# Second set loaded inside the first set's first layer, that layer on 32x32 tiles of TensorE, the sum M on 64x32 tiles, loops written out

## What is computed

```python
def _gn(v):                      # per image and channel
    return (v - mean(v, (1, 2))) / sqrt(var(v, (1, 2)) + 1e-5)

# layer 0: w1 (32, 4), wg (4, 32, 32), w2 (32, 4)
y = gelu(x[..., None] * w1)
z = gelu(einsum('bhwim,moi->bhwmo', y, wg))
out = einsum('bhwmc,cm->bhwc', z, w2)
# layer 1: 4x4 depthwise FIR filter
# layer 2: in windows of 8x8, keys times queries: attn = einsum('bxyhcp,bxyhdp->bxyhcd', q, k) * temperature
# layer 3: weights of 3x3 patches from x itself, scattered back; then batch norm and leaky ReLU
x = x + layer0(_gn(x)); x = x + layer1(_gn(x)); x = x + layer2(_gn(x)); x = x + layer3(_gn(x))
```

## Time and profile before

| | |
|---|---|
| median of 3 runs | 1093.64 us (1091.95 to 1094.71) |
| the profiled execution | 1092.42 us |
| its span | 1090.2 us |
| instructions | 20559 |
| mean granted TensorE clock | 0.845 |
| busy: TensorE, VectorE, ScalarE, GpSimd | 828.1, 821.3, 579.5, 319.2 us |
| data moved | 36.27 MB, 33 GB/s |

### The profile page before, as it was taken

One profiled execution on the slowest core, in us unless ns is written; L12 is line 12 of the kernel. 1 busy time (PEld: TensorE's weight loads), 2 busy tenths in 40 slices (PEclk: granted clock), 3 DMA queues, 4 the chain that ended last, 5 costly groups with the idle time before them and its releaser, 6 DMA issues. The chain is left out here.

```text
span 1090.2 us, 20559 instructions
## 1 busy us (share of the span) xinstructions
PE 828.1 (76%) x6876; PEld 574.6 (53%) x6876; DVE 821.3 (75%) x1165; ACT 579.5 (53%) x615; POOL 319.2 (29%) x233
## 2 busy tenths in 40 slices
PE   5699994979997648635999949979986487445654
PEld 4343334978885448124433319968875384023433
DVE  7577888987876854788577888978758835979993
ACT  5799992333333226445999943323332172525553
POOL 0000006700007940330000029200029900526665
PEclk9799997999998759558899978989998687558686
DMA  9100000000000000225000000000000000003556
GB/s 296 52 0 0 0 0 1 1 1 1 0 0 3 1 20 0 78 65 167 0 0 0 0 0 2 0 2 1 0 1 2 1 20 0 1 0 116 154 155 193
DMA packets 51403, 36.27 MB, mean 33 GB/s; under 512 B 1697, under 2 KB 50977, under 8 KB 51361
## 3 DMA queue, kind: packets, MB, share of 16 engines
q1 hardware_dynamic: 51360, 35.71, 10.7%
HBM read 18.93 MB, written 16.78 MB: 33 GB/s over the span
## 5 line engine op out<-in xcount | busy, mean ns | idle before, releaser
L343 PE MATMUL ps<-work,cst 128*128 128x512 f32 x512 | 237.3, 611 | 17.3 <-ACT work L556 13.5
L343 PEld LDWEIGHTS ps<-work,cst 128*128 128x128 f32 x512 | 94.7, 193 | 158.8 <-issue 144.6
L556 ACT ACTIVATE work<-X,l0s 128x2048 f32 (+1 forms) x64 | 136.7, 2141 | 3.8 <-SPq L303 3.8
L563 ACT ACTIVATE work<-ps 128x2048 f32<-128x2048 f32 x64 | 123.1, 1924 | 8.5 <-PE ps L343 8.3
L999 POOL TENSOR_TENSOR work<-cst,ksum 128x512 f32<-128x512 f32 x64 | 69.6, 1107 | 175.0 <-SPq L303 172.4
L787 DVE TENSOR_TENSOR work<-ps,cst 64x512 f32<-64x512 f32 x128 | 88.2, 689 | 37.1 <-PE ps L410 35.3
L964 POOL TENSOR_TENSOR co<-mv,cst 128x1 f32<-128x1 f32 x8 | 1.5, 191 | 384.5 <-DVEq L250 298.3
L585 ACT ACTIVATE work<-ps 128x512 f32<-128x512 f32 x80 | 47.8, 597 | 98.6 <-PE ps L363 98.6
L374 PE MATMUL ps<-cst,work 128*128 128x143 f32 x640 | 95.9, 294 | 1.4 <-DVE X L737 1.1
L262 PE MATMUL ps<-ST,work 32*128 32x512 f32 x256 | 59.0, 1013 | 45.9 <-DVE work L923 20.4
L707 DVE SCALAR_TENSOR_TENSOR work<-work,cst 128x2048 f32<-128x2048 f32 x32 | 75.2, 2351 | 24.5 <-ACT work L563 24.3
(11 more groups left out here) (96 smaller groups left out, 1548.0 us busy)
## 6 DMA issues: line engine op xcount, KB each, us to landing
work<-x SPq DMA_DIRECT2D x32, 512.0 KB, 4.8
out<-work SPq DMA_DIRECT2D x64, 256.0 KB, 3.2
work<-choose SPq DMA_DIRECT2D x8, 128.0 KB, 2.7
cst<-consts SPq DMA_DIRECT2D x1, 1009.5 KB, 9.2
cst<-consts SPq DMA_DIRECT2D x1, 64.0 KB, 1.9
```

Source lines behind the costliest of these rows:

```text
L343: last = pe.matmul(ps[:, 4 * (m % 2) + b, :], wg[:, m, :], yb[:, m, b * BANK:(b + 1) * BANK], start=True, stop=True)
L556: act.activation(yb[:, m, :], X[:, ds(s * PIX + i * CHUNK, CHUNK)], ACT.Gelu, scale=l0s[:, m:m + 1], bias=l0s[:, MULTI + m:MULTI + m + 1]) ...
L563: act.activation(zb[:, m % 2, :], ps[:, 4 * (m % 2):4 * (m % 2) + 4, :].rearrange("p a b -> p (a b)"), ACT.Gelu).then_inc(s_zs, 1)
```

## The change

- **Load of set 1.** Stage 0 runs for set 0 only. In set 0's stage 1, SP brings set 1 in one-bank pieces (4 columns of the width, 256 KB, two buffers), GpSimd lines each up, TensorE transposes it into bank 6 or 7, VectorE takes its moments and copies it to X. GpSimd works out set 1's scales there too. There is one barrier less.
- **First layer on tiles.** `project_y` uses 16 tiles of 32x32: row tile g is image g, column tile k4 is a quarter of the unit's pixels. z then lies in banks 0 to 3 with one image per bank. There is one such buffer, not two. The products with w2 and the sum over m move from VectorE to TensorE: `weigh_z` multiplies each half unit with diagonal 32x32 matrices (`diag`) on 8 tiles and accumulates in banks 4 and 5. VectorE adds each half chunk of 1024 columns from PSUM to X (`add_half`). `zb` has five buffers, `yb` two.
- **M on 64x32 tiles.** The two windows of a pair go to two row tiles with 33 columns each (32 keys and a one) in place of 128 columns with zeros. `kh` needs no clearing, and the keys' bias is one instruction on 128 partitions.
- **Loops written out.** `Fori` loops become Python loops, so each engine's program is straight. `ksum` lies in the shared work space. The first use of the gelu table is asked for at the end of stage 7.

```diff
-RING, DEEP = 2, 4
+RING, DEEP, ZDEEP = 2, 4, 5
...
-        yb, _e = part(0, [DEEP, CHUNK])
-        zb, _e = part(_e, [RING, CHUNK])
-        acc, _ = part(_e, [CHUNK])
+        yb, _e = part(0, [RING, CHUNK])
+        zb, _e = part(_e, [ZDEEP, G, BANK])
+        stage_b, _e = part(_e, [RING, G, 4 * C])
+        lined_b, _ = part(_e, [RING, 4, G, C])
...
-        kh, _e = part(_e, [RING, 4, G, P])
+        kh, _e = part(_e, [RING, 4, G, C + 1])
 
         rs, _e = part(_e0, [RING, NWIN, P])
-        qb, _ = part(_e, [RING, WS, NWIN // 2, WS])
+        qb, _e = part(_e, [RING, WS, NWIN // 2, WS])
+        ksum = work[:, _e:_e + NWIN * NWIN]
...
-            eng.wait_ge(s_stage, s * (STAGES * ENG) + (k + 1) * ENG)
+            eng.wait_ge(s_stage, (s * (STAGES - 1) + k + 1) * ENG)
...
-                for k in range(STAGES):
+                for k in range(1 if s else 0, STAGES):
+                    if k == 1 and s + 1 < NS:
+                        for n in range(NB):
+                            if n >= RING:
+                                sp.wait_ge(s_lined_b, n - RING + 1)
+                            sp.dma_start(stage_b[:, n % RING, :, :],
+                                         x[(s + 1) * G:(s + 2) * G, :, 4 * n:4 * n + 4, :].rearrange("g h w c -> h g (w c)")
+                                         ).then_inc(s_load_b[n % RING], 16)
                     if k == 5:
                         for r in range(TILES):
                             sp.dma_start(sel[C * r:C * r + C, :, :], choose[0:C, 0:GROUPS, :]).then_inc(s_sel, 16)
-                    if k == 7 and s + 1 < NS:
-
-                        for u in range(LOADS):
-                            load(s + 1, u, u)
...
+                def project_y(i, m):
+
+                    k = s * UNITS + i * MULTI + m
+                    pe.wait_ge(s_y, k + 1)
+                    if k:
+                        pe.wait_ge(s_zs, k)
+                    for k4 in range(4):
+                        for g in range(G):
+                            rows = slice(C * g, C * g + C)
+                            last = pe.matmul(ps[C * k4:C * k4 + C, g, :], wg[rows, m, C * g:C * g + C],
+                                             yb[rows, m % 2, k4 * BANK:(k4 + 1) * BANK], start=True, stop=True)
+                    last.then_inc(s_zp, 1)
+
+                def weigh_z(i, m, hf):
+
+                    n, k = s * (PIX // CHUNK) + i, s * UNITS + i * MULTI + m
+                    pe.wait_ge(s_zs, k + 1)
+                    if m == 0 and 2 * n + hf:
+                        pe.wait_ge(s_x1, 2 * n + hf)
+                    for g in range(G):
                         for b in range(2):
-
-                            pe.wait_ge(s_bank, s * NB + i * 8 + (2 * u + b + 1))
-                            for w in range(4):
-                                one_w = lined[:, u % 2, 4 * b + w, :, :].rearrange("p g c -> p (g c)")
-                                last = pe.transpose(ps[:, 2 * u + b, w * H:(w + 1) * H], one_w, ident)
-                            last.then_inc(s_in, 1)
-                stage_end(pe, s, 0)
-
-
-                with pe.Fori(0, PIX // CHUNK) as i:
-                    for m in range(MULTI):
-                        k = s * UNITS + i * MULTI + m
-                        pe.wait_ge(s_y, k + 1)
-                        pe.wait_ge(s_zs, slot(k))
-                        for b in range(4):
-                            last = pe.matmul(ps[:, 4 * (m % 2) + b, :], wg[:, m, :], yb[:, m, b * BANK:(b + 1) * BANK],
-                                             start=True, stop=True)
-                        last.then_inc(s_zp, 1)
+                            rows = slice(C * (2 * hf + b), C * (2 * hf + b) + C)
+                            last = pe.matmul(ps[C * g:C * g + C, 4 + b, :], diag[rows, m, :], zb[rows, k % ZDEEP, g, :],
+                                             start=(m == 0), stop=(m == MULTI - 1))
+                    if hf or m == MULTI - 1:
+                        last.then_inc(s_w1 if m < MULTI - 1 else s_acc, 1)
+
+                def next_set(n):
+                    if s + 1 < NS:
+                        pe.wait_ge(s_lined_b, n + 1)
+                        if n >= RING:
+                            pe.wait_ge(s_bank_b, n - RING + 1)
+                        for w in range(4):
+                            last = pe.transpose(ps[:, 6 + n % RING, w * H:(w + 1) * H],
+                                                lined_b[:, n % RING, w, :, :].rearrange("p g c -> p (g c)"), ident)
+                        last.then_inc(s_in_b, 1)
+
+                project_y(0, 0)
+                for i in range(PIX // CHUNK):
+                    next_set(4 * i)
+                    if i:
+                        weigh_z(i - 1, 0, 1)
+                    project_y(i, 1)
+                    if i:
+                        for m in range(1, MULTI):
+                            weigh_z(i - 1, m, 1)
+                    next_set(4 * i + 1)
+                    project_y(i, 2)
+                    weigh_z(i, 0, 0)
+                    weigh_z(i, 1, 0)
+                    next_set(4 * i + 2)
+                    project_y(i, 3)
+                    weigh_z(i, 2, 0)
+                    next_set(4 * i + 3)
+                    if i + 1 < PIX // CHUNK:
+                        project_y(i + 1, 0)
+                    weigh_z(i, 3, 0)
+                for m in range(MULTI):
+                    weigh_z(PIX // CHUNK - 1, m, 1)
...
                     for pp in range(4):
-                        for g in range(G):
-                            last = pe.matmul(ps[C * g:C * g + C, 4 + u, pp * P:pp * P + P],
-                                             xw[:, u, pp, C * g:C * g + C], kh[:, u, pp, g, :],
-                                             start=True, stop=True)
+                        for hp in range(2):
+                            rows = slice(N * hp, N * hp + N)
+                            for g in range(G):
+                                last = pe.matmul(ps[C * g:C * g + C, 4 + 2 * u + hp, pp * (C + 1):(pp + 1) * (C + 1)],
+                                                 xw[rows, u, pp, C * g:C * g + C], kh[rows, u, pp, g, :],
+                                                 start=True, stop=True)
                     last.then_inc(s_m, 1)
...
+                def gelu_y(k):
+                    i, m = divmod(k, MULTI)
+                    at = s * 2 * MULTI + m
+                    act.activation(yb[:, k % 2, :], X[:, s * PIX + i * CHUNK:s * PIX + (i + 1) * CHUNK], ACT.Gelu,
+                                   scale=l0s[:, at:at + 1], bias=l0s[:, at + MULTI:at + MULTI + 1]).then_inc(s_y, 1)
+
+                def gelu_z(k):
+                    act.wait_ge(s_zp, s * UNITS + k + 1)
+                    old = s * UNITS + k - ZDEEP
+                    if old >= 0:
+                        n, m = divmod(old, MULTI)
+                        if m < MULTI - 1:
+                            act.wait_ge(s_w1, n * (MULTI - 1) + m + 1)
+                        else:
+                            act.wait_ge(s_acc, 2 * n + 2)
+                    act.activation(zb[:, (s * UNITS + k) % ZDEEP, :, :], ps[:, 0:4, :], ACT.Gelu).then_inc(s_zs, 1)
+
+                gelu_y(0)
+                gelu_y(1)
+                for k in range(UNITS):
+                    gelu_z(k)
+                    if k + 2 < UNITS:
+                        gelu_y(k + 2)
...
-                with dve.Fori(0, PIX // CHUNK) as i:
-                    x_in = X[:, ds(s * PIX + i * CHUNK, CHUNK)]
-                    for m in range(MULTI):
-                        k = s * UNITS + i * MULTI + m
-
-                        dve.wait_ge(s_zs, after(k))
-                        dve.wait_ge(s_x1, slot(k) + 1)
-                        dve.scalar_tensor_tensor(acc if m < MULTI - 1 else x_in, zb[:, m % 2, :],
-                                                 c("w2")[:, m:m + 1], acc if m else x_in, ALU.mult, ALU.add
-                                                 ).then_inc(s_x1, 1)
-                    dve.wait_ge(s_x1, after(k))
-                    alone(dve)
-                    for b in range(4):
-                        dve.bn_stats(stats[:, ds(i * 24 + 6 * b, 6)], X[:, ds(s * PIX + i * CHUNK + b * BANK, BANK)])
+                    dve.bn_aggr(mv_b[:, :], stats_b[:, :]).then_inc(s_aggr_b, 1)
+                add_half(PIX // CHUNK - 1, 1)
                 moments(NB)
...
+                def add_half(i, hf):
+                    n = 2 * (s * (PIX // CHUNK) + i) + hf
+                    at = s * PIX + i * CHUNK + hf * 2 * BANK
+                    dve.wait_ge(s_acc, n + 1)
+                    dve.scalar_tensor_tensor(X[:, at:at + 2 * BANK], ps[:, 4:6, :].rearrange("p a b -> p (a b)"), 1.0,
+                                             X[:, at:at + 2 * BANK], ALU.mult, ALU.add).then_inc(s_x1, 1)
+                    dve.wait_ge(s_x1, n + 1)
+                    alone(dve)
+                    for b in range(2):
```

(47 more changed lines are left out.)

200 lines of the change are left out of this document (106 added, 94 removed).

## The result

The changed kernel takes **1077.09 us** (median of 4 runs, 1075.53 to 1081.78), the kernel before 1092.91; the ratio is 0.986, interval 0.983 to 0.989. The time is 1.4% lower, clear of the spread between runs and inside the range, but the gain is 15.8 us where 48 were forecast. The profiled run is the one of 1075.53.

What follows compares the result with a forecast made beforehand. A chain of barrier-separated stages, each with its own bound: ScalarE in the first layer, TensorE in windows. 1092.4 - 35.2 + 12.4 - 19.8 - 6.4 = 1043.4; the profiled run stands 1.2 under the median, so 1044.6 us, range 1022 to 1084.

Steps and rivals of the forecast that it cites:

- The load stage that goes: Between the sets: set 1's first gelu starts where the load's first copy did, -35.2 us.
- The first layer: First layer of both sets: queueing, head and tail together +8.7 us in set 0 and +3.7 in set 1, +12.4.
- sixteen tiles do run side by side: First-layer projection takes 1.05 us on 16 tiles at once; rival that they don't: 1093 us, chance 0.07.
- the slots: First layer, TensorE's queue between projections: 4.43 and 3.92 us at two places against 3.74; 0.87 lost per set 0 chunk.
- the head: Start of the first layer: the first z needs one y and a projection, 2.3 us gained in each set.
- the cover for the second set's load: First layer: loading set 1 there costs nothing while covered; a 256 KB load may take about 6 us with two buffers.
- tail: End of the first layer, last z to moments: 10.2 us instead of 6.2, +4.0 in each set.
- the clock: Rival: TensorE's clock falls in the first layer; 1115 us at 40% low, chance 0.10; smaller share, 1065 to 1090, 0.08.
- The window stage: TensorE-bound rounds there: M falls from 1.01 to 0.70 us, times 64, -19.8 us; bounds -26 and +11.5.
- the rival of 18.6 ns a pass: Window stage: M is bound by its instructions at L458's rate, M 1.19 us, time 1076; chance 0.10.
- Loops written out: 0: All written-out loops: 0 us, as ScalarE and TensorE keep pace across loop ends and written-out L458 groups run without stall.
- The filter's head: Filter stage start: GpSimd's long memset goes, VectorE's first strip piece falls from 3.80 to 0.6 us, -6.4 us.

Runs made afterwards that it cites:

- the added transposes: Changed kernel with TensorE also transposing old data into banks 6 and 7 in set 1's first layer, in all chunks: 1073.1 and 1077.1 us.
- one wait: Changed kernel with GpSimd's first filter strip held until VectorE's three strip pieces are written: 1064.1 us; filter stage 64.7 / 65.8 instead of 71.0 / 71.3.
- one loop: Changed kernel with GpSimd's 16 rounds of stage 4 as a hardware loop again: 1068.2 us; stage 4 67.2 / 69.3.
- own-banks kernel: Changed kernel with a reordered first-layer end in set 0 and, throughout set 1, second halves in banks 6 and 7, each projection first in its slot: 1054.8 us.

## Why the prediction was wrong

The direction and the largest term were right; the gain was a third of the forecast. The 31.8 us between forecast and span, by the steps of the prediction:

- *The load stage that goes*: right, -35.5 against -35.2.
- *The first layer*: sixteen tiles do run side by side (a projection and its landing in 1.14), the slots and the head came as forecast, and the cover for the second set's load held. The **tail** was sized wrong: +7.3 instead of +4.0 in each set, because the four weightings were priced at the high level behind a wait in which the clock fell (7.08 for 3.7). And in set 1 the rival of **the clock** came true in its small form, 6.7 us of 148; the prediction gave it 0.08. The rest of the layer is 2.5 off; the slots of set 0, 0.18 a chunk longer than forecast (16.01 for 15.83), are part of it.
- *The window stage*: M took 0.69 as taken, and rounds are 2.17; the rival of 18.6 ns a pass doesn't hold. The step that failed is "**Loops written out: 0**", with its sentence that there is no row for a stall by code loading. Blocks of code that come late stop TensorE where a round has 150 instructions in 2.17 us, and 5.9 of the 19.8 were lost. Keeping the loop would not have saved them, since there its turns show as much; the prediction took M's saving as the round's and had no term for the supply of instructions in either form. Its argument from L458, whose groups ran without a stall, carried little: they stand in a stage where TensorE was busy 39.7 of 68.9 us, not 81.7 of 84.0.
- *The filter's head*: the first piece is 0.59 as forecast, the gain 3.2 instead of 6.4. The prediction priced the memset's end and didn't ask **what GpSimd starts next**: its strip came forward, from 5.5 us behind the start of the memset to 0.4, and fell on the next two pieces.
- *Stage 4*: +10.8 against nothing. It is again "Loops written out: 0", and the largest single error: the claim was made from ScalarE's and TensorE's steady rounds, and GpSimd's loop, with its 0.20 us idle ahead of each addition, was not looked at.
- The other stages gave 3.6 that were not forecast; 2.9 of it are stage 7 of the two sets (36.3 and 36.8 instead of 37.9 and 38.1). No run took the cause apart.

What stays open is why the clock falls in set 1. A lack of work on TensorE doesn't explain it (at 1.00 this queue is busy 12.7 of 16 us and fell, the other 10.3 and held), nor does the head. That both the added transposes and the other queue cure it fits an order with waits for VectorE's additions between weightings, which each of them removes or fills; that was not tried by itself.

## What to carry to other kernels

When an engine is freed or its loop overhead goes, look for what it starts next, and against which operation of its port's neighbour that lands: two such collisions cost 14 us here against the forecast, and one wait (11.8) and one loop (9.6) gave 21 back. Cutting matmuls into more and shorter tiles pays until the instructions themselves come too thick: here written-out code cost the steady rounds nothing at 28 and 21 ns an instruction, and did at 14. When an engine stands with nothing to wait for, look for the instruction packets among the transfers. Where TensorE waits at the end of a stage, price what stands behind the wait at the low level too (7.08 us here for 3.7), and give a second half its own banks where any are free: in set 1 that, with the order that it allows, returned 16 us (148.2 to 131.8; 6.0 of it are the end and 6.7 the clock's fall).

## What the runs showed of the hardware

M's 64 passes of 33 columns on eight tiles start within 0.69 us, 10.8 ns apart; the Trainium skill, "TensorE: Matmul & The Clock Gate", in the section on 56 against 53.3 ns, gives about 25 ns as the least between two starts, which doesn't hold for these rows of tiles, and the measurement decides. Each of the 113 stalls of TensorE over 0.3 us in the written-out window stages ended 1.2 to 1.6 us after a packet of instructions had landed. Thirty-two passes of the weighting on sixteen tiles took 1.15 us in set 1 of the own-banks kernel, 16 on eight tiles 1.09 to 1.33 in the changed one: the wider form was nearly free. The same queue at the same place had the clock rise within 16 us in some runs (0.69 to 0.84) and not in others (0.50 to 0.53), worth about 3 us of time from one execution to the next.
